# Group 0 of a tile ahead of the closing sum of the tile before, b1 behind the row stores, and the last stage's stores on GpSimd's queue

## The chip, the core and the metric

The kernel runs on one core of a Trainium2 chip. The metric is the device time of one execution in microseconds (us), as the median of several runs. A core has five engines that run their own instruction streams and meet at semaphores: PE (TensorE, matrix products), DVE (VectorE), ACT (ScalarE), POOL (GpSimd) and SP (SyncE, which here only starts DMA transfers).

## The reference, cut to what matters

A graph attention layer over 6250 nodes of 256 channels (8 heads of 32), with 206,250 edges sorted by destination, and then a layer of 16 experts of which each node takes two. All in float32.

```python
edge_index = jnp.stack([src, dst])
x = x + _L0_gnn_ref(_layernorm(x), edge_index, W, a_src, a_dst, gamma, beta)
x = x + _L0_ffn_ref(_layernorm(x), gate_w, gate_b, w1, b1, w2, b2, gamma, beta)

# _L0_gnn_ref, with its x the normalized rows
hh = (x @ W).reshape(n, H, D)
scores = leaky_relu(s_src[src] + s_dst[dst], 0.2)
m = segment_max(scores, dst)
e = exp(scores - m[dst])
alpha = e / segment_sum(e, dst)[dst]
out = segment_sum(hh[src] * alpha[:, :, None], dst).reshape(n, H * D) + x
return elu(layernorm(out) * gamma + beta)

# _L0_ffn_ref, with its x the normalized rows
topk_vals, topk_idx = top_k(x @ gate_w + gate_b, 2)
topk_w = softmax(topk_vals)
h = relu(einsum('bsh,ehf->bsef', x, w1) + b1)
expert_out = einsum('bsef,efh->bseh', h, w2) + b2
moe = sum(topk_w[..., None] * take(expert_out, topk_idx))
return layernorm(x + moe) * gamma + beta
```

## The kernel before, in words

The 6250 nodes are 49 tiles of 128 (the last has 106). Early stages (0 to 177 us) project the rows, write them with their scores to a table in memory (`table`), and prepare the edge windows. The program is then a row of blocks:

- **The edge stage** (`stage3`, 177 to 2750 us), one turn per node tile. A tile has a window of 34 chunks of 128 edges, taken in four groups of 9, 9, 8 and 8 chunks (`GROUPS`).
- **The last tiles** (`last_tiles`, to 2789.6 us): what is still to be done for the last tiles after the loop.
- **The lists** (`stage5`, to 2803 us), **the experts** (`stage6`, to 3228 us).
- **The last stage** (`stage7`): mixes the two experts' rows of a node, normalizes and stores, in 7 groups of 7 tiles.

*Work of one group in the edge stage.* GpSimd gathers the table rows of each chunk's sources, one indirect DMA per chunk (`gat`, L1265), 34 per tile and one tile ahead of their use. PE looks up the destinations' scores (`look`, L1348, counted by `look_done` once per group). VectorE reduces that (L1394), adds the sources' scores (L1398), takes the maximum (L1400), makes the one-hot matrix `hot` (L1406), and after ScalarE's two exponentials (L1321, L1322) the weighted messages `msg` (L1409). PE then adds `hot` times `msg` into one bank, `ps_sum` (`total`, L1362), over all four groups of a tile; each group's last product counts `sum_done`.

*What must wait for what.* GpSimd takes group g's gathers of the next tile once ScalarE has written its indices (`idx_ready`) and VectorE has made the messages of the same group of this tile (`msg_ready`), which read the old rows; in the middle of a group (k = GROUPS[g] // 2) it also waits for PE's `sum_done` of that group. PE's first product of a tile waits for `added`: VectorE's `num` (L1560), which reads the bank. ScalarE makes the transposed one-hot `hotT` of the next tile (`rows`, L1277 and L1279) in group 3, after the last `look_done` and after the edge row `dst_row` has come in.

*What follows a tile.* `finish` closes it, interleaved with the groups of the next two tiles. VectorE for the tile before: `sums` (num and the first statistics), `scale_inner`, `lift`, `join`. For the tile before that: `scale_outer`, `choose` (top two experts), `place`, `hand_over` (`list_f`, the entries for the experts' lists). ScalarE has the partners `norm_inner` (xn_f), `root_inner` and `root_outer` (std), `centre` (z), `norm_outer` (y), `turned` (yT), `lower`, `odds`. Roots and exponentials lie in different activation tables, so ScalarE loads a table whenever it changes between them. SP sends, per tile, the edge row (`dst_row`, L1243), the edges, the rows `y` (`keep`, L1739) and 16 list pieces (`record`, L1747) once `list_f` is there.

The order on each engine is the order in which the code is written: there is no scheduler. `over_tiles` writes the first and last tiles out and loops over the others.

In `last_tiles`, SP stores the rows y of three tiles and loads the expert biases b1 (L1779). y is one buffer: ScalarE writes a tile's y once the store of the one before has landed (`sent`). In `stage7`, SP issues both the loads of the experts' rows (`back`) and the stores of the result; VectorE waits for `par_in`, the last layer norm's gamma and beta, ahead of its first statistics.

Of the kernel before, what the change touches and what calls it, by code (L numbers as in the profile page):

```python
# [20 lines left out]
ACT = mybir.ActivationFunctionType  # L21
AX = mybir.AxisListType

P = 128
N, D = 6250, 256
# [3 lines left out]
LAST = N - (TILES - 1) * P  # L29
FULL = TILES - 1  # L30
# [3 lines left out]
GRP = 7  # L34
# [1133 lines left out]
def stage3(nc, opening, table, src_pad, dst_pad, dst_half, finish, node_iota, node_id, neg_main, dst_split, lo_i):  # L1168


    with ExitStack() as ctx:
# [99 lines left out]
        def _(act):  # L1271
# [24 lines left out]
            def tile(t, head, old, last=False):  # L1296
                if not last:
                    cast(t + 1)
                if old >= 1:
                    finish.norm_inner(act, t - 1)  # L1300
                    finish.root_inner(act, t - 1)
                    if old >= 2:
                        finish.root_outer(act, t - 2)
                    act.preload_act_table(ACT.Exp)
                for g in range(NG):
                    m, n = g % 2, GROUPS[g]
                    if g == 1 and old >= 1:
                        finish.centre(act, t - 1)
# [3 lines left out]
                    if g == 2 and old >= 1:  # L1312
                        finish.lower(act, t - 1)
# [75 lines left out]
        def _(dve):  # L1389
# [24 lines left out]
            def tile(t, head, old, last=False):  # L1414
                if old >= 1:
                    finish.sums(dve, link, t - 1, ps_sum)
                for g in range(NG):
                    group(t, g, head)
                    if g == 0 and old >= 1:
                        finish.scale_inner(dve, link, t - 1)  # L1420
                    if g == 0 and old >= 2:
                        finish.scale_outer(dve, link, t - 2)
                    if g == 1 and old >= 1:
                        finish.lift(dve, link, t - 1)
                    if g == 1 and old >= 2:
                        finish.choose(dve, link, t - 2, ps_route)
                    if g == 2 and old >= 1:
                        finish.join(dve, link, t - 1)
                    if g == 2 and old >= 2:
                        finish.place(dve, link, t - 2, ps_route, iota)  # L1430
                    if g == NG - 1 and old >= 2:
                        finish.hand_over(dve, t - 2, ps_route)
# [325 lines left out]
def last_tiles(nc, finish, base, taken, w1, w2, b1, w1_sb, w2_sb, b1T, w_in, b1_in, list_constants):  # L1758


    with ExitStack() as ctx:
# [14 lines left out]
        @block.sync  # L1776
        def _(sp):
            finish.keep(sp, a - 1, sp_turn)
            sp.dma_start(b1T[:, :, :].rearrange("p e a -> p (e a)"), b1.rearrange("e (a p) -> p (e a)", p=P)).then_inc(b1_in, 16)  # L1779
            finish.keep(sp, a, sp_turn)  # L1780
            finish.keep(sp, b, sp_turn)
            sp.wait_ge(finish.sent, 16 * TILES)
            sp.wait_ge(finish.listed, 16 * EXPERTS * (a - 1))
# [360 lines left out]
def stage7(nc, fgamma, fbeta, chosen, out, x_all, ident, rstd, nmr, gates):  # L2144


    with ExitStack() as ctx:
# [94 lines left out]
        def _(dve):  # L2242
# [27 lines left out]
            def finish(g):  # L2270
                rows = normed[:, g % 2, :, :]
                dve.wait_ge(norm_ready, g * GRP + GRP)
# [6 lines left out]
            dve.wait_ge(par_in, 32)  # L2279
# [12 lines left out]
        def _(sp):  # L2292
# [21 lines left out]
            sp.dma_start(bet[:, :], fbeta.unsqueeze(0).to_broadcast([P, D])).then_inc(par_in, 16)  # L2314
            for g in range(NGRP):
                if g + 2 < NGRP:
                    load(g + 2)
                sp.wait_ge(out_ready, g + 1)
                t0 = g * GRP
                nt = GRP if g < NGRP - 1 else GRP - 1  # L2320
                sp.dma_start(out[t0 * P:(t0 + nt) * P, :].rearrange("(t p) d -> p t d", p=P),
                             normed[:, g % 2, 0:nt, :]).then_inc(out_sent[g % 2], 16)
            last = (NGRP - 1) % 2
            sp.dma_start(out[FULL * P:N, :], normed[0:LAST, last, GRP - 1, :]).then_inc(out_sent[last], 16)
            sp.wait_ge(out_sent[last], 16 * ((NGRP + 1) // 2 + 1))
            sp.wait_ge(out_sent[1 - last], 16 * (NGRP // 2))
# [21 lines left out]
```

## Time and profile before

| | |
|---|---|
| median of 3 runs | 3359.18 us (3358.12 to 3366.66) |
| profiled execution | 3364.55 us, its span 3362.8 us |
| busy | PE 1790.6 us (53%), VectorE 1683.8 (50%), ScalarE 1018.8 (30%), GpSimd 1840.0 (55%) |
| edge stage, steady loop | 433 to 2708 us |
| one tile there | 52.9 us |
| edge stage to its end | 2750 us |
| last tiles, lists | to 2803 us |
| experts | 2803 to 3228 us |
| last stage | 3228 to 3362.8 us |

The profile is of one execution, which is why its span is set beside its own time and not beside the median. The span is the time between the first and the last instruction; starting and ending the program make up the rest. "Busy" counts the time in which an engine works on an instruction; the idle time ahead of an instruction stands in brackets behind it, with what ended it. "remote" is a releaser that the trace doesn't name; "issue" is time in which the engine waited for nothing that the profile shows. POOL L1265 is the issue of a gather by GpSimd, and SPq or POOLq is the queue of an engine that starts DMAs. In a name such as num<-acc,ps_sum the tile written stands ahead of the arrow; ps_own<-ps_look is the look-up reduction of a group, which the code calls `looked`.

### The profile page before, as it was taken

The numbers are of one execution on the slowest core, as the hardware profiler recorded it, in microseconds if no ns is written. First come the engines' busy times: TensorE is split into PE (matmuls) and PEld (weight loads), VectorE is DVE, ScalarE is ACT, GpSimd is POOL, SyncE is SP. The second block draws the span as 40 slices with busy tenths as digits, with TensorE's granted clock in tenths as the row PEclk, the third lists the DMA queues.
The fourth block names the chain that finished last, engine by engine and source line by source line (L and its number), as shares of the span: only waits on it lengthen the run. The fifth ranks groups of instructions, "written<-read, shape, count | busy, mean of one in ns | idle before, by whom it ended". The sixth has DMA issues, their size and how long they took to land. (4 is left out here: it accounts for less than half of the span.)

```text
span 3362.8 us, 43456 instructions
## 1 busy us (share of the span) xinstructions
PE 1790.6 (53%) x9190; PEld 1462.5 (43%) x9191; DVE 1683.8 (50%) x3940; ACT 1018.8 (30%) x2031; POOL 1840.0 (55%) x1936
## 2 busy tenths in 40 slices
PE   6243544445454454544535444454544535999975
PEld 5132433334343343433434333343433435898964
DVE  6554545545455464554645445454554542333346
ACT  4232323233232332323233232332323312333442
POOL 2455656566565666656566565665656523555520
PEclk9676777777677776777767777776777767999987
DMA  5443434434343343433434344343443436333343
GB/s 185 114 116 98 122 103 125 116 106 119 105 123 116 107 119 105 123 110 115 117 105 123 102 125 117 107 119 103 124 118 106 119 82 205 101 103 101 106 142 130
DMA packets 184424, 393.55 MB, mean 117 GB/s; under 512 B 52129, under 2 KB 106810, under 8 KB 178116
## 3 DMA queue, kind: packets, MB, share of 16 engines
q0 software_dynamic: 92288, 267.12, 27.9%
q1 hardware_dynamic: 75876, 111.73, 10.7%
q10 hardware_dynamic: 16224, 14.30, 1.5%
q8 instruction: 13, 0.21, 0.0%
q14 instruction: 23, 0.19, 0.0%
HBM read 356.52 MB, written 36.47 MB: 117 GB/s over the span
## 5 line engine op out<-in xcount | busy, mean ns | idle before, releaser
L1265 POOL DMA_INDIRECT gat<-table,idx x1632 | 1547.0, 948 | 999.0 <-issue 452.5
L1362 PE MATMUL ps_sum<-msg,hot 128*128 128x264 f32 x3332 | 1076.1, 493 | 1049.3 <-DVE msg L1409 779.1
L1362 PEld LDWEIGHTS ps_sum<-msg,hot 128*128 128x128 f32 x3332 | 815.2, 250 | 1252.2 <-issue 1067.0
L1409 DVE TENSOR_TENSOR msg<-gat,ps_weight 128x2304 f32<-128x2304 f32 x196 | 473.5, 2416 | 399.9 <-ACT ps_weight L1321 391.0
L1560 DVE TENSOR_TENSOR num<-acc,ps_sum 128x264 f32<-128x264 f32 x49 | 21.0, 430 | 692.4 <-remote 681.5
L1277 ACT ACTIVATE hotT<-dst_row,neg_id 128x4352 bf16<-128x4352 int16 x48 | 188.3, 3922 | 285.3 <-remote 271.8
L1679 ACT ACTIVATE std<-var 128x1 f32<-128x1 f32 x49 | 9.9, 203 | 832.7 <-DVE var L1571 824.1
L1406 DVE TENSOR_TENSOR hot<-ps_own,rel 128x1152 f32<-128x1152 f32 x196 | 251.0, 1281 | 0.0
L1348 PE MATMUL ps_look<-dst_split,hotT 128*128 (+1 forms) x1666 | 80.9, 191 | 280.5 <-ACT hotT L1279 266.0
L2089 PE MATMUL ps_ht<-xT,w_t 128*128 128x128 f32 x1712 | 215.0, 280 | 2.0 <-DVE w_t L2122 1.6
L2089 PEld LDWEIGHTS ps_ht<-xT,w_t 128*128 128x128 f32 x1712 | 202.9, 194 | 6.9 <-DVE w_t L2122 4.6
L2013 POOL DMA_INDIRECT chosen<-o_sb,put_at x105 | 114.3, 1088 | 155.6 <-DMA chosen<-o_sb,put_at 70.2
L2098 PE MATMUL ps_o<-w_sb,hidT 128*128 x840 | 198.8, 380 | 0.0
L1348 PEld LDWEIGHTS ps_look<-dst_split,hotT 128*128 128x128 bf16 x1666 | 67.3, 101 | 298.8 <-issue 276.0
L1279 ACT ACTIVATE hotT<-hotT 128x4352 bf16<-128x4352 bf16 x48 | 183.8, 3829 | 1.5
L2098 PEld LDWEIGHTS ps_o<-w_sb,hidT 128*128 128x128 f32 x840 | 151.8, 191 | 16.2
L2004 POOL DMA_INDIRECT xt<-y_rows,get_at x111 | 110.0, 991 | 52.3 <-issue 28.0
L2052 ACT ACTIVATE hidT<-ps_ht,b1T 128x128 f32<-128x128 f32 x424 | 121.2, 369 | 43.7 <-issue 43.7
L1394 DVE TENSOR_REDUCE ps_own<-ps_look 128x144 f32<-128x432 f32 x196 | 115.0, 587 | 12.0 <-remote 10.2
L2122 DVE COPY w_t<-w_sb 128x1024 f32 x108 | 75.7, 701 | 78.3 <-issue 68.3
L2046 ACT ACTIVATE xT<-ps_x 128x256 f32<-128x256 f32 x108 | 41.5, 384 | 211.2 <-PE ps_x L2080 195.7
L1703 ACT ACTIVATE yT<-ps_t_f 128x256 f32<-128x256 f32 x47 | 18.1, 384 | 243.5 <-PE ps_t_f L1712 132.0
(395 smaller groups left out, 2049.7 us busy)
## 6 DMA issues: line engine op xcount, KB each, us to landing
dst_row<-dst_half SPq DMA_DIRECT2D x49, 1088.0 KB
gat<-table,idx POOLq DMA_INDIRECT x1666
b_t<-in_L_ffn_b_dram ACTq DMA_DIRECT2D x107, 128.0 KB
w_sb<-in_L_ffn_w_dram SPq DMA_DIRECT2D x6, 2048.0 KB, 12.5
listing<-list_f SPq DMA_DIRECT2D x736, 0.5 KB
back<-chosen SPq DMA_DIRECT2D x5, 1792.0 KB, 10.0
table<-rows SPq DMA_DIRECT2D x49, 128.0 KB, 1.7
y_rows<-y SPq DMA_DIRECT2D x49, 128.0 KB
```

Source lines behind the costliest of these rows:

```text
L1265: pool.indirect_dma_start(gat[:, GSTART[g] + k, :], None, table, bass.IndirectOffsetOnAxis(ap=idx[g][:, k:k + 1], axis=0)).then_inc(landed ...
L1277: act.activation(hotT[:, :], dst_row[:, :], ACT.Abs, bias=neg_id[:, bass.ds(t, 1)]).then_inc(apart_ready, 1)
L1279: act.activation(hotT[:, :], hotT[:, :], ACT.Relu, bias=1.0, scale=-1.0).then_inc(hotT_ready, 1)
L1348: last = pe.matmul(ps_look[m][:, k * SPLIT * 2 * HEADS:(k + 1) * SPLIT * 2 * HEADS], by_chunk[:, GSTART[g] + k, :], dst_split[:, bass.ds(t ...
L1362: last = pe.matmul(ps_sum[:, 0:SUM], hot[:, m, k, :], msg[:, m, k, :], start=(g == 0 and k == 0), stop=(g == NG - 1 and k == n - 1))
L1394: dve.tensor_reduce(looked[:, 0:n, :], ps_look[m][:, 0:n * SPLIT * 2 * HEADS].rearrange("p (j c h) -> p j h c", c=SPLIT, h=2 * HEADS), AX. ...
L1406: dve.tensor_tensor(hot[:, m, 0:n, :], iota.unsqueeze(1).to_broadcast([P, n, P]), rel[:, j:j + n].unsqueeze(2).to_broadcast([P, n, P]), AL ...
L1409: dve.tensor_tensor(msg[:, m, 0:n, 0:D].rearrange("p j (h d) -> p j h d", d=HD), gat[:, j:j + n, 0:D].rearrange("p j (h d) -> p j h d", d=HD),
L2013: pool.indirect_dma_start(chosen, bass.IndirectOffsetOnAxis(ap=put_at[:, s:s + 1], axis=0), o_sb[:, o, :], None).then_inc(o_out, 16)
L2052: last = act.activation(hidT[:, s, j * P:(j + 1) * P], ps_ht[s][:, j * P:(j + 1) * P], ACT.Relu, bias=b1T[:, bass.ds(e, 1), j:j + 1].rearr ...
L2089: last = pe.matmul(ps_ht[o][:, j * P:(j + 1) * P], w1_t[:, o, a, j * P:(j + 1) * P], xT[:, o, a * P:(a + 1) * P], start=(a == 0), stop=(a ...
L2098: last = pe.matmul(ps_o[o][:, 0:D], hidT[:, o, j * P:(j + 1) * P], w2_sb[:, bass.ds(e, 1), j, :].rearrange("p a b -> p (a b)"), start=(j = ...
```

## The change

Three parts. In the edge stage, VectorE does the whole of a tile's group 0 ahead of `sums` of the tile before, and the steps behind it move on by a group: `scale_inner` behind group 1, `lift` behind group 2, `join` behind group 3. ScalarE's steps follow: `root_outer` stands alone ahead of group 0 and `root_inner` ahead of group 1, each followed by a load of the table of exponentials; `centre` goes to group 2 and `lower` to group 3. In `last_tiles`, b1 is loaded behind the three row stores. In the last stage, the stores of the result are issued by GpSimd and not by SP, and VectorE waits for gamma and beta only ahead of its first use of them.

```diff
--- before.py
+++ after.py
@@ -1298,18 +1298,20 @@
                     cast(t + 1)
                 if old >= 1:
                     finish.norm_inner(act, t - 1)
-                    finish.root_inner(act, t - 1)
-                    if old >= 2:
-                        finish.root_outer(act, t - 2)
+                if old >= 2:
+                    finish.root_outer(act, t - 2)
                     act.preload_act_table(ACT.Exp)
                 for g in range(NG):
                     m, n = g % 2, GROUPS[g]
                     if g == 1 and old >= 1:
-                        finish.centre(act, t - 1)
+                        finish.root_inner(act, t - 1)
+                        act.preload_act_table(ACT.Exp)
                     if g == 1 and old >= 2:
                         finish.norm_outer(act, t - 2)
                         finish.turned(act, t - 2, ps_t)
                     if g == 2 and old >= 1:
+                        finish.centre(act, t - 1)
+                    if g == NG - 1 and old >= 1:
                         finish.lower(act, t - 1)
                     if g == 2 and old >= 2:
                         finish.odds(act, t - 2)
@@ -1412,22 +1414,22 @@
                                   ALU.mult).then_inc(msg_ready, 1)
 
             def tile(t, head, old, last=False):
-                if old >= 1:
-                    finish.sums(dve, link, t - 1, ps_sum)
                 for g in range(NG):
                     group(t, g, head)
-                    if g == 0 and old >= 1:
-                        finish.scale_inner(dve, link, t - 1)
                     if g == 0 and old >= 2:
                         finish.scale_outer(dve, link, t - 2)
+                    if g == 0 and old >= 1:
+                        finish.sums(dve, link, t - 1, ps_sum)
                     if g == 1 and old >= 1:
-                        finish.lift(dve, link, t - 1)
+                        finish.scale_inner(dve, link, t - 1)
                     if g == 1 and old >= 2:
                         finish.choose(dve, link, t - 2, ps_route)
                     if g == 2 and old >= 1:
-                        finish.join(dve, link, t - 1)
+                        finish.lift(dve, link, t - 1)
                     if g == 2 and old >= 2:
                         finish.place(dve, link, t - 2, ps_route, iota)
+                    if g == NG - 1 and old >= 1:
+                        finish.join(dve, link, t - 1)
                     if g == NG - 1 and old >= 2:
                         finish.hand_over(dve, t - 2, ps_route)
 
@@ -1776,9 +1778,9 @@
         @block.sync
         def _(sp):
             finish.keep(sp, a - 1, sp_turn)
-            sp.dma_start(b1T[:, :, :].rearrange("p e a -> p (e a)"), b1.rearrange("e (a p) -> p (e a)", p=P)).then_inc(b1_in, 16)
             finish.keep(sp, a, sp_turn)
             finish.keep(sp, b, sp_turn)
+            sp.dma_start(b1T[:, :, :].rearrange("p e a -> p (e a)"), b1.rearrange("e (a p) -> p (e a)", p=P)).then_inc(b1_in, 16)
             sp.wait_ge(finish.sent, 16 * TILES)
             sp.wait_ge(finish.listed, 16 * EXPERTS * (a - 1))
 
@@ -2269,6 +2271,8 @@
 
             def finish(g):
                 rows = normed[:, g % 2, :, :]
+                if g == 0:
+                    dve.wait_ge(par_in, 32)
                 dve.wait_ge(norm_ready, g * GRP + GRP)
                 link(dve.tensor_tensor(rows, rows, spread_tiles(gam[:, :]), ALU.mult))
                 link(dve.tensor_tensor(rows, rows, spread_tiles(bet[:, :]), ALU.add))
@@ -2276,7 +2280,6 @@
 
             gate_diag(0)
             gate_diag(1)
-            dve.wait_ge(par_in, 32)
             for g in range(NGRP):
                 if g >= 1:
                     scale(g - 1)
@@ -2312,18 +2315,21 @@
             load(1)
             sp.dma_start(gam[:, :], fgamma.unsqueeze(0).to_broadcast([P, D])).then_inc(par_in, 16)
             sp.dma_start(bet[:, :], fbeta.unsqueeze(0).to_broadcast([P, D])).then_inc(par_in, 16)
+            for g in range(2, NGRP):
+                load(g)
+
+        @block.gpsimd
+        def _(pool):
             for g in range(NGRP):
-                if g + 2 < NGRP:
-                    load(g + 2)
-                sp.wait_ge(out_ready, g + 1)
+                pool.wait_ge(out_ready, g + 1)
                 t0 = g * GRP
                 nt = GRP if g < NGRP - 1 else GRP - 1
-                sp.dma_start(out[t0 * P:(t0 + nt) * P, :].rearrange("(t p) d -> p t d", p=P),
-                             normed[:, g % 2, 0:nt, :]).then_inc(out_sent[g % 2], 16)
+                pool.dma_start(out[t0 * P:(t0 + nt) * P, :].rearrange("(t p) d -> p t d", p=P),
+                               normed[:, g % 2, 0:nt, :]).then_inc(out_sent[g % 2], 16)
             last = (NGRP - 1) % 2
-            sp.dma_start(out[FULL * P:N, :], normed[0:LAST, last, GRP - 1, :]).then_inc(out_sent[last], 16)
-            sp.wait_ge(out_sent[last], 16 * ((NGRP + 1) // 2 + 1))
-            sp.wait_ge(out_sent[1 - last], 16 * (NGRP // 2))
+            pool.dma_start(out[FULL * P:N, :], normed[0:LAST, last, GRP - 1, :]).then_inc(out_sent[last], 16)
+            pool.wait_ge(out_sent[last], 16 * ((NGRP + 1) // 2 + 1))
+            pool.wait_ge(out_sent[1 - last], 16 * (NGRP // 2))
 
 
 # ---- launch: one core; inputs and outputs as the reference has them ----
```

VectorE at the head of the loop, before: behind the two rows that close the loop over tiles stands what follows a turn, num (`sums`) first and the look-up reduction of group 0 eight rows later.

```order
L1669 COPY list_f<-ps_route 16x128
L1217 REGISTER_ALU
L1217 COMPARE_AND_BRANCH
L1560 TENSOR_TENSOR num<-acc,ps_sum 128x264
L1562 TENSOR_SCALAR rden<-num 128x8
L1563 RECIPROCAL rden<-rden 128x8
L1564 TENSOR_TENSOR num<-num,rden 128x256
L1566 TENSOR_TENSOR num<-num,xn_f 128x256
L1568 BN_STATS stats<-num 128x6
L1570 BN_AGGR mv<-stats 128x2
L1571 TENSOR_SCALAR var<-mv 128x1
L1394 TENSOR_REDUCE ps_own<-ps_look 128x144
```

VectorE at the same place, now:

```order
L1671 COPY list_f<-ps_route 16x128
L1217 REGISTER_ALU
L1217 COMPARE_AND_BRANCH
L1396 TENSOR_REDUCE ps_own<-ps_look 128x144
L1400 TENSOR_TENSOR both<-gat,ps_own 128x144
L1402 TENSOR_REDUCE score<-both 128x72
L1408 TENSOR_TENSOR hot<-ps_own,rel 128x1152
L1411 TENSOR_TENSOR msg<-gat,ps_weight 128x9x256
L1599 RECIPROCAL rstd<-std 128x1
L1600 SCALAR_TENSOR_TENSOR nmr<-mv,rstd 128x1
L1562 TENSOR_TENSOR num<-acc,ps_sum 128x264
```

Group 0's five instructions and the two of `scale_outer` now stand ahead of num; line numbers are two higher, since the code above them is two lines longer.

ScalarE at the same place, before (std of `root_inner` and `root_outer` side by side, then the table of exponentials; z is `centre`, y and yT are `norm_outer` and `turned`):

```order
L1674 ACTIVATE xn_f<-x_all,nmr,rstd 128x256
L1679 ACT_TABLE_LOAD
L1679 ACTIVATE std<-var 128x1
L1683 ACTIVATE std<-var 128x1
L1304 ACT_TABLE_LOAD
L1321 ACTIVATE ps_weight<-score 128x72
L1322 ACTIVATE msg<-score 128x9x8
L1687 ACTIVATE z<-num,nmr,rstd 128x256
L1698 ACTIVATE y<-x_all,nmr,rstd 128x256
L1703 ACTIVATE yT<-ps_t_f 128x256
```

ScalarE now:

```order
L1676 ACTIVATE xn_f<-x_all,nmr,rstd 128x256
L1685 ACT_TABLE_LOAD
L1685 ACTIVATE std<-var 128x1
L1303 ACT_TABLE_LOAD
L1323 ACTIVATE ps_weight<-score 128x72
L1324 ACTIVATE msg<-score 128x9x8
L1681 ACT_TABLE_LOAD
L1681 ACTIVATE std<-var 128x1
L1308 ACT_TABLE_LOAD
L1700 ACTIVATE y<-x_all,nmr,rstd 128x256
L1705 ACTIVATE yT<-ps_t_f 128x256
```

A tile has four table loads where it had two, and z has gone behind group 1's exponentials.

SP in `last_tiles`, before:

```order
L1739 DMA y_rows<-y 128x256
L1779 DMA b1T<-in_L_ffn_b_dram 128x64x1
L1739 DMA y_rows<-y 128x256 x2
```

SP there now:

```order
L1741 DMA y_rows<-y 128x256 x3
L1783 DMA b1T<-in_L_ffn_b_dram 128x64x1
```

All three row stores stand ahead of b1.

## Rows read from the trace of the kernel before

**Rows 1.** Steady loop: us, busy time of each engine (instructions), TensorE clock, DMA share, GB/s
```profile
433.41:2707.80 2274.39, 1077.60 (x5030) 847.28 (x5030) 1188.11 (x2580) 660.05 (x1117) 1385.68 (x1462) 0.73 0.40 114
```
**Rows 2.** Uses of num, 1005 to 2695 us: ns min/median/max, first and last start
```profile
L1560 DVE TENSOR_TENSOR num<-acc,ps_sum x32: 428/430/431, 1015.0 to 2655.7; 128x264 f32<-128x264 f32 x32
```
**Rows 3.** Waits in the steady loop: us in total, times, longest us
```profile
DVE num L1560 <- remote: 610.4, 43, 14.3
...
POOL gat L1265 <- DVE msg L1409: 158.5, 85, 3.4
```
**Rows 4.** Timeline of VectorE, one tile: start us, us, what [idle before <-releaser]
```profile
1226.64 0.43 DVE L1560 TENSOR_TENSOR num<-acc,ps_sum 128x264 f32<-128x264 f32 x1 [14.26 <-remote]
...
1229.49 0.62 DVE L1394 TENSOR_REDUCE ps_own<-ps_look 128x144 f32<-128x432 f32 x1
...
1234.82 0.16 DVE L1597 RECIPROCAL rstd<-std 128x1 f32 x1
...
1265.54 0.27 DVE L1669 COPY list_f<-ps_route 16x128 f32<-16x128 f32 x1
```
**Rows 5.** Timeline of PE, the same tile
```profile
1210.00 0.54 PE L1348 MATMUL ps_look<-dst_split,hotT 128*128 x9 [6.08 <-ACT hotT L1279]
1212.29 5.70 PE L1362 MATMUL ps_sum<-msg,hot 128*128 128x264 f32 x16 [1.75 <-issue]
...
1234.69 6.88 PE L1362 MATMUL ps_sum<-msg,hot 128*128 128x264 f32 x18 [16.41 <-DVE msg L1409]
...
1245.03 4.24 PE L1362 MATMUL ps_sum<-msg,hot 128*128 128x264 f32 x18 [1.75 <-issue]
...
1287.95 5.87 PE L1362 MATMUL ps_sum<-msg,hot 128*128 128x264 f32 x18 [15.65 <-DVE msg L1409]
```
**Rows 6.** Timeline of GpSimd, the same tile
```profile
1202.49 0.95 POOL L1265 DMA_INDIRECT gat<-table,idx  x1 [2.63 <-remote]
...
1227.32 0.94 POOL L1265 DMA_INDIRECT gat<-table,idx  x1 [3.83 <-remote]
...
1242.39 0.95 POOL L1265 DMA_INDIRECT gat<-table,idx  x1 [2.29 <-PE ps_sum L1362]
...
1255.93 0.94 POOL L1265 DMA_INDIRECT gat<-table,idx  x1 [2.56 <-remote]
...
1280.56 0.95 POOL L1265 DMA_INDIRECT gat<-table,idx  x1 [3.62 <-remote]
```
**Rows 7.** Timeline of ScalarE, the same tile
```profile
1229.88 1.28 ACT L1304 ACT_TABLE_LOAD   x1
...
1255.40 3.92 ACT L1277 ACTIVATE hotT<-dst_row,neg_id 128x4352 bf16<-128x4352 int16 x1 [5.74 <-remote]
```
**Rows 8.** Timeline of SyncE's DMA queue, the same tile
```profile
1215.87 26.08 SPq L1747 DMA_DIRECT2D listing<-list_f  x16
1243.65 0.16 SPq L1243 DMA_DIRECT2D dst_row<-dst_half  x1
```
**Rows 9.** 1245.0 to 1249.3 us, columns as in rows 1
```profile
1245.00:1249.30 4.30, 4.27 (x26) 3.62 (x27) 3.54 (x16) 0.72 (x3) 3.38 (x4) 1.00 0.93 290
```
**Rows 10.** The line that loads b1 (L1779)
```profile
DMA to landing us min/median/max: 24.2/24.2/24.2
```
**Rows 11.** Timelines of ScalarE and GpSimd in the stage of the last tiles
```profile
2776.62 0.60 ACT L1698 ACTIVATE y<-x_all,nmr,rstd 128x256 f32<-128x256 f32 x1 [13.89 <-DMA y_rows<-y]
...
2783.76 1.58 POOL L1663 DMA_INDIRECT listing<-ids,at_i  x1 [13.29 <-DVE at_i L1652]
```
**Rows 12.** Timelines of PE and SyncE's queue in the last stage
```profile
3242.09 0.70 PE L2237 MATMUL ps_moe<-back,diag 128*128 128x256 f32 x2 [1.63 <-DVE stats L2256]
...
3265.28 1.22 PE L2237 MATMUL ps_moe<-back,diag 128*128 128x256 f32 x2 [4.79 <-DVE stats L2256]
...
3356.29 0.41 SPq L2324 DMA_DIRECT2D out_dram<-normed  x1
```
**Rows 13.** The chain that ended last: start us, us, what
```profile
3312.98 13.10 DMA back<-chosen
```

## The prediction

> **What bounds the kernel now.** I read the stretches of time first. The steady loop of the edge stage fills 433 to 2708 us, two thirds of the span, and no engine is near full there: GpSimd leads with 1386 of 2274 us for 1462 gathers, 0.95 us each [rows 1]. The closing sum (num) starts 32 times between 1015.0 and 2655.7: one tile in 52.9 us [rows 2]. Gathers in a row start 1.25 us apart (1242.39 to 1255.93 - 2.56 is eight such steps and one of 0.95 [rows 6]), so 34 of them need 42.6. Some 10 us of a tile are GpSimd standing still. The list of waits names VectorE's 43 waits before num, up to 14.3 us and of unknown source, and GpSimd's for messages, up to 3.4 [rows 3].
>
> The timelines of one tile give the mechanism. PE's last group starts at 1212.29 and its 16 passes end 5.70 us later, 1217.99 [rows 5]. Yet VectorE sits until 1226.64 [rows 4] and GpSimd until 1227.32, both waiting for that one count [rows 6]. The same a half tile later: PE's second group ends at 1249.27 [rows 5], but ScalarE (hotT needs the look-ups that come right behind it) and GpSimd go on at 1255.40 and 1255.93 [rows 6, 7]. PE's counts are held back, and what the two places have in common is a GpSimd in the middle of an unbroken run of gathers; they come once it stands still. From the start of a run to the release it is 1226.6 - 1202.5 = 24.1 us for 17 gathers, 1255.4 - 1242.4 = 13.0 for 9: some 1.42 us per gather. A count made in the first few us of a run is not held: the copy list_f at 1265.54 needs PE's list and starts without idling, in a run that goes from 1255.93 on to 1280.56 - 3.62 = 1276.94 [rows 4, 6]. The two that were held were made 6.9 us or more into a run.
>
> Call F the release (1226.5). Then: sums 2.9 us (to 1229.49) and group 0 5.1 on VectorE [rows 4]; PE's first group from 1234.69 = F+8.2 [rows 5]; GpSimd goes on with its fifth gather behind it at 1242.39 = F+15.9, or F+14.9 where PE's first group takes 5.87 us and not 6.88 [rows 5, 6]. From there to the next F all is set by runs of 9 and 17 gathers: (1280.56 - 0.8) - 1242.39 = 37.4 us [rows 6].
>
> **The change, part 1: group 0 ahead of the sums.** Nothing is added on VectorE; 14 us of its idle time seem to wait for group 0. But group 0 needs the counts of look-up (look_done), which PE makes at 1210.5 [rows 5], 8 us into GpSimd's run of 17 [rows 6], and in order with the others. I take it as held too. So VectorE starts group 0 at F, not before: 5.1 us, then scale_outer (two instructions of 0.16 us, 0.4 with their gap), then num, 0.43 [rows 4]. PE needs num alone (`added`), which empties its bank: its first group starts at F+6.1 instead of F+8.2. The other 2.5 us of sums now run beside PE. GpSimd finds the messages of group 0 at F+5.9, just as its four gathers end (F+5.8), so the 3.4 us wait goes [rows 3]; it halts at F+10.7 and needs PE's first group: F+13.0 or F+12.0. It resumes 0.8 later, 2.0 us earlier than before. PE starts colder or not by chance: granted clock is at 1.2 GHz (0.5) when it starts after its pause, and the two forms of the group differ by 1.0 us [rows 5]; for this I take off 0.1. Gain 1.9 us a tile, x 47 tiles with such a release = 89 us.
>
> What is late next? ScalarE gets two table loads more (1.28 us each [rows 7]): one pair lies before F where it idles, the other ends near F+10.0, y at F+10.7, before PE can use it (F+12.0). Join and its 2.3 us move behind group 3, so hand_over comes 2.4 us later and SP's 16 listing DMAs with it (26.1 us, then dst_row, 1088 KB, at 1243.65 [rows 8]). The DMA engines are 93% busy at 290 GB/s until 1249.3 [rows 9], so I take dst_row as landed near 1249 and hotT has it 6.2 us early. That cover loses 2.4 and 2.0 and still has about 2. The ring behind it is the floor: listing to dst_row 27.8 us, landing 5.2, two hotT passes 7.8, then 2.6 to the end of list_f (1265.81) [rows 4, 7, 8], join 2.3, and from list_f to the next listing 3.3 (1215.87 + 53.24, the period of rows 6, - 1265.81): 49.0 against the 51.0 that I forecast.
>
> **Part 2: b1 behind the rows.** b1 is read in 4-byte pieces and takes 24.2 us to land [rows 10]; the row store of tile 47 stands behind it in SP's queue, and ScalarE waits 13.89 us for that store before the last tile's y at 2776.62 [rows 11]. Moved, y starts when ScalarE comes free, at 2762.7. The rest of that block hangs on it; GpSimd's other scatters end at 2783.76 - 13.29 = 2770.5 [rows 11], so its last two start then: 13 us. b1 is issued near 2763 now and lands by 2787 even if it again takes 24.2 us; the expert stage, which moves up to 2790, reads it only behind its first products. Bounds: 0 (it collides with the scatters and gathers that follow) to 13.9.
>
> **Part 3: last stage.** The parameter wait leaves ahead of the first statistics: PE's 1.63 us go [rows 12]. Loads no longer queue behind out_ready; the last one takes 13.1 us from issue to PE [rows 13] and could go some 10 us earlier, as soon as PE has finished the group whose buffer it takes. But a PE that runs ahead stops for VectorE's 12 us of a group all the more often, and after such a stop it starts slow: 1.22 us for two passes after 4.79 us of idling, 0.70 after 1.63 [rows 12]. So I count 3 us for the loads. Against it the stores by GpSimd: waking takes 0.8 and issuing 0.95, as for a gather [rows 6], against 0.41 on SP [rows 12], which stands twice at the end: +1.5 to +2.5. By my count -1.6 - 3 + 2.1 = -2.5, bounds -16 (all loads free, PE fast) and +3 (nothing but the dearer stores).
> The Trainium skill (DMA: Bandwidth & Descriptors, Specifications) gives GpSimd's queue about 1 us to the first byte and the sync queue 0.6, and says under "Issuing engines are not separate DMA queues" that spreading issue over engines saves issue time only. By it the last store lands 0.4 us later and the bandwidth stays; no trace here yet shows a store of GpSimd's in this stage.
>
> **Sum.** -89 - 13 - 2.5 = -104.5 us against the profiled execution's 3364.55: 3260. That execution lies 5.4 above the median of the runs (3359.18), so the forecast for the median is 3255.
>
> **Rivals.**
> - Look-ups not held. Group 0 then really runs in the gap, num follows F at once, PE starts at F+0.6; its end falls into GpSimd's run of 8 and waits for the drain, F+12.1, GpSimd resumes at F+12.9. Gain 2.5 a tile, 118 in all: 3225. For it: no waiter shows when look-up counts arrive. Against: PE's counts come in order, and later ones are held. 0.12.
> - No hold at all, once VectorE isn't waiting. Then a tile costs GpSimd's 42.6 + 0.8: 9.5 x 47 = 447 less, about 2900. 0.02. A page's rule points there: the Trainium skill (TensorE: Matmul & The Clock Gate, "The cost: per-tile semaphore tail") prices a count of PE in tens of ns; the trace has 8.5 us between PE's end and its waiter [rows 4, 5], so it disagrees.
> - The run of 8 is held longer. After 17 gathers GpSimd stood 3.83 us, after 9 it was 2.56 [rows 6]; without its 0.8 to wake, the release came 3.0 and 1.8 us behind the last gather. With 3.0 here it is F+13.7, GpSimd resumes at F+14.5: gain 0.9 a tile, 3359 - 42 - 15.5 = 3301.5, say 3301. 0.14.
> - Slower: the list falls into the hold. If PE's list matmul comes more than some 5 us into GpSimd's run (I work out 2), hand_over waits for F, SP's listing starts at F+3.6, dst_row lands at F+36.6, hotT ends F+44.4, messages of group 3 at F+46.9, PE's sum at F+53.5. It keeps itself up, since place waits for the listing. +0.6 a tile, +28 - 15.5: 3372. For it: SP's 26.1 us; against: in each tile before, the list came in time. 0.10.
>
> **How the numbers follow.** Forecast 0.62, its own range 3235 to 3280 (gain per tile 1.5 to 2.3, last stage +3 to -16). Rivals 0.12, 0.02, 0.14, 0.10. The range for 8 in 10 reaches over the first and most of the third: 3212 to 3320. This kernel's measurement can't tell less than 0.3% (10 us) from no change. Faster: 0.62 + 0.12 + 0.02 + 0.12 = 0.87 or so; same 0.05; slower 0.08.
>
> **What would show it.** num to num in 51.0 us in the steady loop; VectorE's idle time moved from before num to before group 0's look-up reduction, still of unknown source and some 11 us long; PE's first group 6.1 us after that wait ends; GpSimd in runs of 8, 9 and 17 with no wait for messages. ScalarE's 13.9 us before the last y gone. If the reduction of group 0 follows list_f directly, the look-ups aren't held; if hand_over idles, the last rival holds; if the tile takes 52 us or more, the hold after 8 gathers is longer than I think.

## The result, and the profile after

The changed kernel takes 3494.34 us (median of 4 runs, 3491.96 to 3521.41), the kernel before 3362.92 in the same session (4 runs, 3358.12 to 3367.52): 1.0409 times as long, 95% interval 1.0386 to 1.0432. The forecast was 3255. The profiled execution took 3494.87 us, with a span of 3493.1.

| | before | after | forecast |
|---|---|---|---|
| up to the last tiles' block | 2750.6 us | 2895.9 | about 2662 |
| from there to the experts' first gather | 53.9 | 44.8 | 40.9 |
| experts | 423.9 | 422.6 | as before |
| last stage | 134.4 | 129.9 | 131.9 |

All of the loss lies in the edge stage, +145 us. The two stretches of parts 2 and 3 gained 9.1 and 4.5 us, 13.6 in all where 15.5 were forecast. The steady loop of the changed kernel, columns as in [rows 1], and num as in [rows 2]:

```profile
440.00:2850.00 2410.00, 1125.17 (x4992) 869.93 (x4990) 1179.02 (x2562) 768.79 (x1190) 1380.42 (x1457) 0.72 0.38 107
```
```profile
L1562 DVE TENSOR_TENSOR num<-acc,ps_sum x32: 428/428/430, 1006.9 to 2758.0; 128x264 f32<-128x264 f32 x32
```

From the first num of the 32 to the last it is 1751.1 us over 31 tiles, 56.5 us each, where [rows 2] give 52.9. The busy times are nearly as before but for ScalarE's table loads, so the tile is longer by waiting. The list of waits from 500 to 2800 us (us in total, times, longest) names two waits that [rows 3] don't have, ScalarE's for the edge row and VectorE's before the logits, and GpSimd's for messages have grown; num's 610 us are gone:

```profile
ACT hotT L1277 <- DMA dst_row<-dst_half: 364.3, 38, 15.9
...
DVE logits L1605 <- remote: 325.1, 30, 13.6
POOL gat L1265 <- DVE msg L1411: 293.1, 55, 11.7
```

The timelines of one tile, SyncE's queue first, then VectorE, ScalarE and GpSimd; they answer to [rows 8], [rows 4], [rows 7] and [rows 6]:

```profile
1217.01 32.84 SPq L1749 DMA_DIRECT2D listing<-list_f  x16
1252.72 0.02 SPq L1243 DMA_DIRECT2D dst_row<-dst_half  x1
...
1271.40 35.78 SPq L1749 DMA_DIRECT2D listing<-list_f  x16
```
```profile
1215.76 0.27 DVE L1671 COPY list_f<-ps_route 16x128 f32<-16x128 f32 x1
1216.17 0.62 DVE L1396 TENSOR_REDUCE ps_own<-ps_look 128x144 f32<-128x432 f32 x1
...
1221.69 0.43 DVE L1562 TENSOR_TENSOR num<-acc,ps_sum 128x264 f32<-128x264 f32 x1
...
1244.70 0.17 DVE L1605 COPY logits<-ps_route 128x16 f32<-128x16 f32 x1 [12.18 <-remote]
...
1265.94 2.29 DVE L1411 TENSOR_TENSOR msg<-gat,ps_weight 128x2048 f32<-128x2048 f32 x1 [9.16 <-ACT ps_weight L1323]
...
1270.15 0.27 DVE L1671 COPY list_f<-ps_route 16x128 f32<-16x128 f32 x1
```
```profile
1258.01 3.92 ACT L1277 ACTIVATE hotT<-dst_row,neg_id 128x4352 bf16<-128x4352 int16 x1 [5.18 <-DMA dst_row<-dst_half]
```
```profile
1214.64 0.95 POOL L1265 DMA_INDIRECT gat<-table,idx  x1 [6.20 <-DVE msg L1411]
...
1245.66 0.95 POOL L1265 DMA_INDIRECT gat<-table,idx  x1 [3.80 <-remote]
```

These steps form a ring: each waits for the one before, and the last leads back to the first, so that one turn is the period of a tile. From list_f at 1215.76, 1.25 us to the first piece, 32.84 for sixteen of them, 2.87 to dst_row, 5.29 until it has landed and hotT starts, 7.93 to the messages of group 3, 4.21 for these and join, and list_f again at 1270.15: 54.4 us. This tile is a short one. Over 41 tiles of the trace the same six steps have means of 1.25, 33.2, 4.2, 5.6, 7.9 and 4.2 us, 56.4 in all, which is the whole period. Sixteen pieces took 26.08 us in [rows 8]. Over 42 tiles of each trace, the time from the first piece's issue to the last's has a median of 26.0 us (25.1 to 26.8) before and 33.4 (19.2 to 36.0) after.

Why the pieces take longer shows when the same queue is cut at GpSimd's runs. In the changed kernel GpSimd runs from 1214.64 to 1241.9 with one stop of 1.3 us. Here is SyncE from 1217 to 1229, and from 1229 to 1244.5:

```profile
1217.01 10.93 SPq L1749 DMA_DIRECT2D listing<-list_f  x8
```
```profile
1230.54 9.85 SPq L1749 DMA_DIRECT2D listing<-list_f  x3
```

Eight pieces in 10.9 us, then three in 9.9. The kernel before has the same thing in a shorter stretch. This is its SyncE from 1215 to 1226.5 and then from 1226.5 to 1243:

```profile
1215.87 10.53 SPq L1747 DMA_DIRECT2D listing<-list_f  x3
```
```profile
1226.82 15.13 SPq L1747 DMA_DIRECT2D listing<-list_f  x13
```

So SyncE is delayed in the same stretch as PE's counts, the back part of a run of gathers: some 3.5 to 5 us a piece in place of 1.2. Before, list_f came 9.6 us into a run of 17 gathers (1265.54 - 1255.93, [rows 4, 6]), and GpSimd stopped 11.4 us later; only 3 of 16 pieces fell into the slow stretch. In the changed kernel list_f and GpSimd's restart both follow the messages of group 3, so list_f comes 1.1 us into a run (1215.76 - 1214.64), and the run goes on for 26.1 us more (21 gathers). So it is in 22 of 41 tiles of the trace; in the others a stop of over 2 us cuts it sooner. In the median tile 6 of the 15 steps between pieces are longer than 2 us, where before there were 2.

For the small parts, ScalarE and GpSimd in the stage of the last tiles (to be held against [rows 11]), and GpSimd in the last stage (against [rows 12]):

```profile
2908.38 0.60 ACT L1700 ACTIVATE y<-x_all,nmr,rstd 128x256 f32<-128x256 f32 x1 [0.41 <-DVE nmr L1600]
```
```profile
2916.09 1.58 POOL L1665 DMA_INDIRECT listing<-ids,at_i  x1 [0.30 <-DVE at_i L1654]
2917.97 1.56 POOL L1665 DMA_INDIRECT listing<-ids,at_i  x1 [0.30 <-issue]
2929.87 0.99 POOL L1879 DMA_INDIRECT ids_f<-listing,row_i  x1 [10.35 <-DVE row_i L1913]
...
3486.49 0.85 POOL L2327 DMA_DIRECT2D out_dram<-normed  x1 [8.94 <-DVE normed L2279]
3487.33 0.62 POOL L2330 DMA_DIRECT2D out_dram<-normed  x1
```

The 13.9 us wait before y is gone, and GpSimd's scatters follow each other.

### The profile page after: what moved, and what is told of

It is laid out like the page before. It is cut to its first block and busy times, and to the rows that moved or that the text cites. A ratio compares the mean times of both kernels' runs of the same rounds, so it can differ in the third digit from the quotient of the medians.

```text
span 3493.1 us, 43595 instructions
## 1 busy us (share of the span) xinstructions
PE 1854.7 (53%) x9190; PEld 1496.6 (43%) x9191; DVE 1686.3 (48%) x3940; ACT 1150.2 (33%) x2125; POOL 1849.5 (53%) x1944
## 5 line engine op out<-in xcount | busy, mean ns | idle before, releaser
L1364 PE MATMUL ps_sum<-msg,hot 128*128 128x264 f32 x3332 | 1096.7, 500 | 415.0 <-issue 248.4
L1364 PEld LDWEIGHTS ps_sum<-msg,hot 128*128 128x128 f32 x3332 | 830.2, 255 | 622.4 <-issue 432.3
L1605 DVE COPY logits<-ps_route 128x16 f32<-128x16 f32 x47 | 8.0, 171 | 366.2 <-remote 366.2
L1709 ACT ACTIVATE ediff<-diff 128x1 f32<-128x1 f32 x49 | 9.9, 203 | 395.1 <-DVE diff L1610 388.6
L1722 PE MATMUL ps_route<-gw,yT 128*128 128x16 f32 x188 | 42.9, 346 | 181.3 <-issue 119.2
L2006 POOL DMA_INDIRECT xt<-y_rows,get_at x111 | 111.2, 1002 | 50.9 <-issue 28.0
L2054 ACT ACTIVATE hidT<-ps_ht,b1T 128x128 f32<-128x128 f32 x424 | 121.2, 368 | 44.8 <-issue 44.8
L1727 PE MATMUL ps_route<-both_h,before 128*128 128x16 bf16 x47 | 8.8, 188 | 225.8 <-DVE both_h L1615 224.0
L1722 PEld LDWEIGHTS ps_route<-gw,yT 128*128 128x128 f32 x188 | 38.2, 284 | 186.2 <-issue 185.4
```

The source lines that it names most:

```text
L1364: last = pe.matmul(ps_sum[:, 0:SUM], hot[:, m, k, :], msg[:, m, k, :], start=(g == 0 and k == 0), stop=(g == NG - 1 and k == n - 1))
L2054: last = act.activation(hidT[:, s, j * P:(j + 1) * P], ps_ht[s][:, j * P:(j + 1) * P], ACT.Relu, bias=b1T[:, bass.ds(e, 1), j:j + 1].rearr ...
```

## The experiments

The chips differ, and every reading depends on it. On some the kernel before takes 3362 to 3367 us, as above; there PE's counts are held. On others it takes 2853 us, and nothing is held. I call them chips of the first and of the second kind. All ratios are to the kernel before on the same chip.

**Batch 1, second kind.**

e1, parts 2 and 3 alone:

```diff
             finish.keep(sp, a - 1, sp_turn)
-            sp.dma_start(b1T[:, :, :].rearrange("p e a -> p (e a)"), b1.rearrange("e (a p) -> p (e a)", p=P)).then_inc(b1_in, 16)
             finish.keep(sp, a, sp_turn)
             finish.keep(sp, b, sp_turn)
+            sp.dma_start(b1T[:, :, :].rearrange("p e a -> p (e a)"), b1.rearrange("e (a p) -> p (e a)", p=P)).then_inc(b1_in, 16)
...
```

The rest of its edit is the change's own in the last stage.

> The kernel before with parts 2 and 3 of the change alone (b1 behind the row stores; last stage). In the changed kernel's trace the stretch from the last tiles' first load to the first gather of the experts is 9.1 us shorter (44.75 for 53.9) and the last stage 4.5 us (129.9 for 134.4). My theory, that all of the loss comes from the reordered edge stage: 13.6 us less than before, about 3349. Rival, that b1's transfer or GpSimd's stores cost something once the edge stage is as it was: 3363 or more.

2839.51 us against 2853.54, ratio 0.9956 (0.9939 to 0.9973): the 13.6 us expected came as 14 (8 to 17 by the interval), though from 2853 and not from 3363.

e2, the changed kernel with the row ahead of the pieces, on SP:

```diff
-                if not head:
-                    lo = window(t)
-                    sp.wait_ge(hotT_ready, t)
-                    sp.sem_inc(sp_turn, 1)
-                    sp.dma_start(dst_row[:, :], dst_half[bass.ds(lo, WIN)].unsqueeze(0).to_broadcast([P, WIN])).then_inc(row_in, 16)
                 if not last:
                     edges(t + 1)
                 if old >= 3:
-                    finish.record(sp, t - 3, sp_turn)
+                    finish.keep(sp, t - 3, sp_turn)
+                if not last:
+                    row(t + 1)
+                if old >= 3:
+                    finish.pieces(sp, t - 3, sp_turn)
```

`row(t)` holds the five lines taken away, and `pieces` is `record` without `keep`.

> The changed kernel, but SP sends the edge row of the next tile (dst_row) ahead of the 16 list pieces and not behind them. My theory is a ring through SP: list_f, 16 pieces (33 to 36 us where they were 26), dst_row, hotT, messages of group 3, join, list_f. With dst_row out of it ScalarE no longer waits for the row, and a tile should go from 56.5 us to 51 or 52: about 3494 - 47 x 5 = 3260. Rival one, that the new order on VectorE and ScalarE is itself the loss (table loads, join later): within 20 us of 3494. Rival two, that the pieces remain the ring without the row (place waits for the pieces of the tile before): a tile of 53 to 55 us, 3330 to 3420.

e3, the same swap on the kernel before:

> The kernel before with the same swap on SP. There ScalarE waits for PE's held counts and the row is 6 us early, so my theory says no change: 3363, plus or minus 5. If the row's arrival mattered there too, a tile would be up to 6 us shorter: down to 3100.

e4, the changed kernel with list_f ahead of join:

```diff
-                    if g == NG - 1 and old >= 1:
-                        finish.join(dve, link, t - 1)
                     if g == NG - 1 and old >= 2:
                         finish.hand_over(dve, t - 2, ps_route)
+                    if g == NG - 1 and old >= 1:
+                        finish.join(dve, link, t - 1)
```

> The changed kernel with hand_over (list_f) ahead of join on VectorE, so 2.3 us earlier behind group 3. Ring through SP: each tile is at least 2.3 us shorter, 108 us in all, about 3386, more if the pieces then lie better against GpSimd's runs. Rival, the order of the other steps is the loss: no change, 3494.

e2 2845.75 (0.9961, 0.9946 to 0.9977), e3 2853.74 (0.9994, 0.998 to 1.0009), e4 2844.76 (0.9961, 0.9945 to 0.9977). None of the expectations of times applied, since the baseline itself was 500 us lower. The trace of e3, whose order on the engines is that of the kernel before but for SP, shows what is missing there. VectorE's num, GpSimd's gather that waits for the same count, and PE's group:

```profile
1211.81 0.43 DVE L1565 TENSOR_TENSOR num<-acc,ps_sum 128x264 f32<-128x264 f32 x1 [6.68 <-PE ps_sum L1367]
```
```profile
1211.98 0.95 POOL L1270 DMA_INDIRECT gat<-table,idx  x1 [0.30 <-PE ps_sum L1367]
```
```profile
1205.04 6.63 PE L1367 MATMUL ps_sum<-msg,hot 128*128 128x264 f32 x16 [4.51 <-DVE msg L1414]
```

PE's group ends at 1211.67 and num starts 0.14 us later, while GpSimd goes on without a gap. In [rows 4, 5] the same took 8.65 us. A slower TensorE is not what held the count in [rows 5]: its 16 passes took 5.70 us there, and 6.63 here, where the count came at once. GpSimd is the bound here: 1332 us of gathers in 1760, which with the steps of 1.25 us is all of the time.

```profile
440.00:2200.00 1760.00, 1037.54 (x4818) 814.97 (x4818) 1135.26 (x2478) 644.12 (x1071) 1332.15 (x1405) 0.79 0.49 141
```

**Batch 2, second kind.** e5, the changed kernel again, and e6, ScalarE's new order with VectorE's old one (its edit is the first part of the change on ScalarE, and nothing else); then e7, part 1 alone.

> The changed kernel itself, once more. On the chip of e1 to e4 the kernel before takes 2854 us and a tile 42.6 us: GpSimd's 34 gathers stand end to end, PE's counts arrive in 0.1 us in the middle of a run and SP's pieces are 1.21 us apart all the time. If the same conditions hold here, both orders are bound by GpSimd and only parts 2 and 3 count: 11 to 13 us less than before, about 2842. If the conditions of the first traces hold (before 3363), the changed kernel is 4% slower again: about 3494. Rival, for the fast conditions: the later join costs here too, a tile over 43 us, 2860 or more.

> The kernel before with ScalarE's new order alone (root_inner in front of group 1, centre in group 2, lower in group 3, two more table loads a tile); VectorE's order as before. Under the conditions of the first traces (before 3363): my theory of the ring through SP says hand_over stays where it was, so the pieces and the row too, and the loss is small, below 50 us (group 1's exponentials wait for root_inner's table loads, and z comes later); the rival that ScalarE's order is the loss says +100 or more. Where before takes 2854: no difference over 5 us.

> The reordered edge stage alone, b1 and the last stage as before. Where the kernel before takes 2853 us: no change but 0 to 10 us either way, since GpSimd's gathers are the bound. Where it takes 3363: my theory of the ring through SP says +145 (the edge stage of the changed kernel is 145 us longer than before's), 3508; the rival, that the loss needs parts 2 or 3, says 3363.

e5 2842.27 (0.9962, 0.9945 to 0.9979), e6 2851.50 (0.9998, 0.9988 to 1.0007), e7 2854.31 in its one run against 2857.06. On these chips the reordering makes no difference that can be seen, and the gain is that of parts 2 and 3. SyncE is not slowed: the issues of a piece in e5 and, below it, in the first trace of the changed kernel (ns min/median/max):

```profile
L1749 SPq DMA_DIRECT2D listing<-list_f x736: 257/258/298, 271.0 to 2210.5; - x184
```
```profile
L1749 SPq DMA_DIRECT2D listing<-list_f x736: 2/257/1402, 310.7 to 2880.2; - x184
```

**Batch 3, first kind.** I had meant to imitate the slow pieces on a chip of the second kind, and the runs came to one of the first. One edit for all four: a second register load ahead of each piece.

```diff
         for e in range(EXPERTS):
+            sp.value_load(self.base_i[0:1, e:e + 1], min_val=0, max_val=DROWS - P)
             at = sp.value_load(self.base_i[0:1, e:e + 1], min_val=0, max_val=DROWS - P)
```

> The kernel before, with one more register load ahead of each of SP's 16 list pieces, whose value is not used: about 0.8 us a piece, so that a piece takes 2.0 us, as in the changed kernel's first trace, where it took 1.2 otherwise. Ring through SP in this order: list_f, pieces (32 us), dst_row (1.7), landing 5, hotT 7.8, messages 2.6, list_f, 1.3 to the first piece: about 50.5 us a tile, 2853 + 47 x 7.9 = 3225 where the kernel before takes 2853. Rival, that SP has slack enough: 2853.

> The changed kernel with the same slowed pieces. The ring has join in it as well, 2.3 us: 52.8 us a tile, about 3320, and 95 above the slowed kernel before. Rival, that the order makes no difference to the ring: as the slowed kernel before, less 11.

> The changed kernel with slowed pieces and dst_row sent ahead of them. The row is out of the ring, and 16 pieces of 2.0 us fit into GpSimd's 42.6 us: about 2845. If the pieces themselves are the ring (place waits for those of the tile before): 3000 or more.

> The changed kernel with slowed pieces and hand_over ahead of join: join is out of the ring, so as the slowed kernel before less parts 2 and 3, about 3212. Rival: no change against the slowed changed kernel.

| with slowed pieces | us | ratio to before (3362.38) |
|---|---|---|
| s1, order before | 3480.89 | 1.035 (1.0283 to 1.0418) |
| s2, changed | 4028.94 | 1.198 (1.1941 to 1.2019) |
| s3, changed, row first | 3528.54 | 1.0492 (1.0385 to 1.0599) |
| s4, changed, list_f ahead of join | 3924.62 | 1.167 (1.1525 to 1.1815) |

The absolute times missed by far (I had reckoned from 2853). Of the order, it came true that s2 is the slowest and that sending the row first takes most of the loss back. It did not that s3 would be the fastest of the four, nor that s4 would be level with s1: s3 is 48 us above s1, and s4 444 above it. The same edit costs 118 us in the old order and 535 in the new one (from the 3494 of the result, on another chip), and moving one transfer takes 500 of these back. The waits of s1, s2 and s3 (500 to 2900 us):

```profile
ACT hotT L1277 <- DMA dst_row<-dst_half: 584.9, 36, 20.2
```
```profile
ACT hotT L1277 <- DMA dst_row<-dst_half: 750.5, 36, 27.6
```
```profile
DVE base_i L1638 <- DMA listing<-list_f: 451.5, 36, 18.0
```

Slowed pieces make ScalarE wait for the row in the old order too. With the row out of the way, the longest wait of s3 is the second way round: place waits for the pieces of the tile before. The 104 us from s2 to s4 are 2.2 a tile, near join's 2.3, but with two runs of each (s4's lie 41 us apart) the size is rough.

**Batch 4, first kind.** e8, e9 and e10 have the edits of e2, e4 and e3, and e11 has both swaps.

> The changed kernel with dst_row sent ahead of the list pieces (as e2). Where before takes 3363: the ring theory says ScalarE's waits for the row (364 us in the steady loop) go and a tile falls from 56.5 us to 51 to 53: 3240 to 3340. If the pieces alone make the ring: 3400 or more. Rival, that the order on VectorE and ScalarE is the loss: about 3494. Where before takes 2853: 2845 again.

> The changed kernel with hand_over ahead of join (as e4). Where before takes 3363: join's 2.3 us leave the ring, 108 us or more less than the changed kernel's 3494: 3386 or below; if join is not in the ring, 3494. Where before takes 2853: 2845 again.

> The kernel before with dst_row ahead of the pieces (as e3). Where before takes 3363: the row was in time there and VectorE, ScalarE and GpSimd wait for PE's held counts, so 3363 plus or minus 10; if the row mattered, 3300 or less.

> The changed kernel with both swaps, the row ahead of the pieces and hand_over ahead of join. Where before takes 3363: neither is in the ring, and if a tile then takes the 51.0 us of my forecast, 3255; I expect it to be no slower than e8 and below 3330. Where before takes 2853: about 2842.

| | us | ratio to before (3366.76) |
|---|---|---|
| e8, changed, row first | 3250.68 | 0.9656 (0.9628 to 0.9684) |
| e9, changed, list_f ahead of join | 3315.17 | 0.9852 (0.98 to 0.9905) |
| e10, before, row first | 3361.97 | 0.9982 (0.9969 to 0.9994) |
| e11, changed, both | 3254.61 | 0.9655 (0.9629 to 0.9682) |

e8 beats the kernel before on both kinds of chip, by 3.4% here and by 0.4% on the second kind (e2), where it is level with the changed kernel. It has the whole new order of VectorE and ScalarE, so neither that order nor its table loads are the loss: the row behind the pieces is. The swap is worth some 240 us in the new order (3494 less 3251, on different chips) and hardly anything, 5 us, in the old one. Moving join out of the ring alone (e9) gives 179 us against the changed kernel's 3494, 3.8 a tile. Of these, 2.0 are join itself, out of the ring. Most of the rest is that SyncE gets to the row sooner behind its last piece (2.2 us for 4.2 in the mean), while the pieces are 0.9 us shorter in the mean (a median of 31.9 us for 33.4) and the row lands 0.7 us later. So it isn't join's delay of list_f that stretched them from 26. In e8 the row goes out before the pieces, which are still slow (nine in the 24.9 us shown), and hardly anybody waits for them (VectorE 51 us, in 13 waits, in the whole execution). Here are SyncE, then VectorE's longest wait in the loop:

```profile
1227.45 0.35 SPq L1242 DMA_DIRECT2D dst_row<-dst_half  x1
1234.34 24.91 SPq L1753 DMA_DIRECT2D listing<-list_f  x9
```
```profile
DVE logits L1610 <- remote: 563.9, 41, 15.0
```

**Batch 5, second kind.** These were meant for the first kind, so they don't tell what they were to tell.

> The kernel before with ScalarE's new order alone (as e6). Where before takes 3363: list_f keeps its place, so by the ring through SP the loss is small, 0 to 30 us; by the rival that ScalarE's order is the loss, 3460 or more. Where before takes 2853: 2851 again.

> Parts 2 and 3 alone (as e1). Where before takes 3363: 13.6 us less, 3349, by the stretches of the changed kernel's trace. Rival: no gain, 3363.

> The changed kernel, for comparison on the same chip. Where before takes 3363: 3494 plus or minus 30, since its tiles are irregular (51 to 61 us in the trace). Where before takes 2853: 2842 again.

e12 2850.66 (0.9998, 0.998 to 1.0016), e13 2838.13 (0.9955, 0.994 to 0.9969), e14 2846.91 (0.9979, 0.9961 to 0.9996), before 2852.86. They repeat e6, e1 and e5. ScalarE's new order alone was not run on a chip of the first kind; that it isn't the loss there rests on e8. The changed kernel was not timed a second time on a chip of the first kind; its loss there rests on the 4 runs of the result, and its cause on s1 to s4 and e8 to e11, on two chips of that kind.

## Why the prediction was wrong

- **What bounds the kernel.** Right on the first kind of chip: PE's counts are held in the back part of a run of gathers and come when GpSimd stops. But it isn't a property of the kernel alone: on the second kind a count reached its waiter 0.14 us after the group's end in the middle of an unbroken run. What differs between the chips, and why counts are late beside GpSimd's gathers, stayed open; no experiment reached it. One trace could not have shown it. The 2900 worked out under "No hold at all" is near what the kernel before takes there, 2853. The rule of the Trainium skill (TensorE: Matmul & The Clock Gate, "The cost: per-tile semaphore tail") that a count costs tens of ns fits the second kind of chip (0.14 us with the waiter's own start) and not the first (8.65 us).
- **"What is late next?", the failed step.** The sum took SP's 16 pieces as 26.1 us wherever they stand, and the step from the listing to dst_row as 27.8. They were 26 us where GpSimd stopped 11.4 us behind list_f. In the back part of a run SyncE issues a piece in 3.5 to 5 us, not 1.2, and in the new order list_f stands at the start of a run, 1.1 us into it, and no longer near its end. That made it 33.2 us for the pieces in the mean (33.4 in the median) and 4.2 more to the row, 37.4 in place of 27.8. The first step, 3.3 us to the listing, was 1.25. With these two the floor that I had worked out at 49.0 becomes 56.6 (49.0 + 9.6 - 2.0), and the tile took 56.5. So the edge row, which I had in time with about 2 us to spare, is what ScalarE waits for, 364 us in 38 waits. The 2.4 us by which join delays list_f are not what stretched the pieces: e9, where they are gone, still has 31.9 us for them. The floor was in the text, term by term, and 2 us short of the forecast; the row that showed its longest term bending (3 pieces in 10.5 us, then 13 in 15.1) was to be had from the trace of before by cutting the same timeline in two.
- **Group 0 ahead of the sums.** The size was right once the row was out of the ring: e8 has 50.9 us a tile and 3250.7 us, where 51.0 and 3255 were forecast. The way was not quite the forecast's. I had group 0 start at F with the look-ups held. In e8 and in the changed kernel the look-up reduction follows list_f with no wait (1216.17 above), as in the first rival, because hotT and with it PE's look-ups now fall ahead of a GpSimd run (changed kernel, 1211.64 against 1214.64) or near its start (e8, 1227.31 against 1225.86). What is held in their place is the count of the logits, which VectorE awaits for up to 15 us; before, PE made the logits at the start of a run (1242.34, the run from 1242.39) and VectorE did not wait, and I had not followed that count. GpSimd still stops three times a tile, for 8.3 us over its 42.6. That e8 hits the forecast within 5 us is therefore in part chance.
- **The slower rival.** It had SP's list in the right place but the wrong mechanism: list_f was not held, the pieces behind it were slow. At +0.6 us a tile it was mis-sized sixfold against +3.6, and it too kept the pieces at 26 us.
- **Part 2.** y's wait went and the scatters closed up, 13 us in the stage itself; but the wait before the listing is read grew from 6.2 to 10.4 us, and the whole way to the first gather of the experts is 9.1 shorter. It grew in the same way between e6 and e13 (6.4 to 11.2 us). The most likely cause is b1's small pieces, issued at 2909.46 next to the scatters, which was the named bound; no run took b1 out, so this is not shown.
- **Part 3.** 4.5 us for 2.5. PE restarts slow in nearly every group, 1.22 us for two passes after 4.79 us of idling, as said. The stores by GpSimd cost less: the last one is issued 1.1 us after VectorE's end (3487.33 - 3486.21), where SP took 0.45; I had counted 2.1 in all.

## What to carry to other kernels

A duration read from a queue belongs to the place where the instructions stand: before a step is moved, cut the timeline of every engine behind it at the neighbours' bursts, and see whether it runs at one pace. A ring that has 2 us of slack on 51 is a rival with a price of its own. The cheap cure, here sending the one transfer that somebody waits for ahead of sixteen that nobody does, is found from the same sum. And one trace is one chip: a wait that ends with an unknown releaser should be seen on a second chip before a tuning rests on it.

## What the runs showed of the hardware

- The same program took 3363 us on some chips and 2853 us on others, in the median; a tile of the edge stage took 52.9 us on the first and 42.6 us on the second (e3's trace). Batches 1, 2 and 5 ran on four chips of the second kind, batches 3 and 4 on two of the first.
- Where counts are held, SyncE's own instructions are slow too, register loads and arithmetic among them, not DMA issues alone: in the changed kernel a DMA issue of a piece took up to 1402 ns, where 298 to 313 ns is the longest in every trace of the second kind, for the same 736 instructions.
- In that stretch SyncE's instructions don't slow down evenly but start in steps of 0.70 us: 1229.12, 1229.83, 1230.54 and 1231.27 for an address calculation, a move, a DMA issue and a register load. The pieces' instructions in the changed kernel have 857 gaps near 0.70 us and 283 near 1.40; in e5 they have 44 and none. The 4.95 us between two DMA issues of pieces (1230.54 and 1235.49) are seven such steps. The profiled execution of the kernel before (3364.55 us) lies among the others (3358 to 3367), which speaks against the recording as the cause, but no run tests it.
- On a chip of the second kind GpSimd issued gathers 1.25 us apart without a stop, and neither PE's counts nor SyncE showed it.
